# Five of eight state products on GpSimd, row replication in fp32, residual and biases on TensorE

## The chip, the cores and the metric

One core of a Trainium2 chip runs the whole program in one launch. Its engines are TensorE (PE, matmuls from SBUF to PSUM), VectorE (DVE), ScalarE (ACT), GpSimd (POOL) and SyncE (SP, which issues most DMAs). The metric is the time of one execution on the device in microseconds; lower is better.

## The reference

The input is x of 2 x 16 x 16 x 64, so 2 batches of 256 tokens with 64 features. Six layers follow one another: an edge attention with an MLP, a group-normalised attention, an attention with 8 heads, a mixture of 8 experts with top 2, six state-space layers, and a second mixture. The change touches the six state-space layers (and small pieces of work that are slipped in before them):

```python
def selective_scan(u, dt, A, Bm, Cm, Dp):
    def step(h, inp):
        u_t, dt_t, B_t, C_t = inp
        h = jnp.exp(dt_t[..., None] * A) * h + (dt_t * u_t)[..., None] * B_t[:, None, :]
        y_t = jnp.einsum('bds,bs->bd', h, C_t)
        return (h, y_t)
    ...
def mamba_mixer(x, in_w, cw, cb, xp_w, dt_w, dt_b, A_log, Dp, out_w):
    xz = x @ in_w
    u, z = jnp.split(xz, 2, axis=-1)
    uc = silu(causal_conv4(u, cw) + cb)
    x_dbl = uc @ xp_w                            # 16 for dt, 16 for B, 16 for C
    dt = jax.nn.softplus(dt_r @ dt_w + dt_b)
    A = -jnp.exp(A_log)
    y = selective_scan(uc, dt, A, Bm, Cm, Dp)
    y = y * jax.nn.silu(z)
    return y @ out_w
for i in range(6):
    residual = hidden if residual is None else hidden + residual
    hidden = rmsnorm(residual, norm_w[i])
    hidden = mamba_mixer(hidden, ...)
```

Inner width is 128 channels, the state has 16 entries per channel, the sequence is 256 steps.

## The kernel before

Every engine has its own instruction stream, written out by hand, and semaphores order the streams. The state-space part is twelve *units* u = 0 to 11, unit u being layer u // 2 of batch u % 2. The two batches alternate, so that while the scans of unit u run, unit u+1 is prepared. Units 0 and 9 to 11 are written out; units 1 to 8 come from a loop of two turns over four units.

A unit holds 16 states, taken in four groups g of four states: a group is a tile of 128 channels x (4 x 256). For each group there is a *drive* product (dt times u, times B, replicated over the channels), a scan over 1024 columns with the decay factors, and a *weighing* product with C. Eight products thus.

- DVE (`v_step`): `prep_dt` (L1091: two polynomial steps L1098, a product L1102, dt L1105, dtu L1108), `gate` of the unit before (L1085), drive of group 0 (L1121, B from PSUM), `residual` of the unit before (L1089), four scans (L1133), and the weighings of groups 0, 2 and 3 (L1140, C from PSUM); `prep_uc` of the next unit (L1078) stands after the third scan.
- POOL (`p_step`): drives of groups 1 to 3 (L1611, B from a DMA broadcast), weighing of group 1 (L1619), and small operations for the next unit: the root mean square, the scaling of the hidden state (L1567), gz (L1576), parts of softplus's polynomial (L1597, L1600), and the rounding remainders (L1582, L1588).
- PE (`pe_step`): B and C must be replicated over 128 channels. The kernel holds them as three bf16 parts stacked on 96 rows and multiplies with a picking matrix: `spread_b` (L634) and `spread_c` three times (L643), each four matmuls of 256 columns into two PSUM banks (4 and 5). `sum_y` (L664) adds the weighed states in PSUM by fp32 matmuls with the identity, sixteen a unit; `sum_skip` (L650) adds D times u. `prep_transpose`, `prep_in`, `prep_x` and `prep_dt` (L609 to L627) prepare the next unit; `out_proj` (L672) is the output projection; `keep_awake(3)` (L655) are three matmuls without use.
- ACT (`a_step`): sixteen decay exponentials (L1405), the norm's squares (L1353), ht in two halves (L1361), two sigmoids by tanh (L1368, L1373), copies xds and stack (L1377, L1379), softplus: abs, relu, exp and four squares (L1385 to L1391), and the middle part of the stack (L1397).
- SP: per unit it writes xds to a scratch tensor in device memory and reads it back as four broadcasts to 128 partitions (three groups of B, group 1 of C), 512 KB each; and it reloads one layer's weights every second unit.

An fp32 matmul shows as two records on PE. PE, DVE, ACT and POOL each run their stream in order.

Of the kernel before, what the change touches and what calls it, by code (L numbers as in the profile page):

```python
# [19 lines left out]
P = 128  # L20
# [15 lines left out]
LOG1P = np.polynomial.Polynomial(  # L36
    np.polynomial.chebyshev.Chebyshev.interpolate(
        lambda u: np.log1p(u) / np.maximum(u, 1e-300), 8, domain=[0, 1]).convert(
        kind=np.polynomial.Polynomial).coef)

def quadratics():
    roots = LOG1P.roots()
    upper = sorted((r for r in roots if r.imag > 0), key=lambda r: r.real)
    k2 = float(LOG1P.coef[-1]) ** (1.0 / len(upper))
    k = k2 ** 0.5
    return [(k, -k * r.real, k2 * r.imag ** 2) for r in upper]
# [29 lines left out]
def hybrid(nc, x, const, w0, w1, w2, w3, w5, wm, rows, out):  # L77
    ctx = ExitStack()
    with ctx:
# [3 lines left out]
        spill = nc.dram_tensor("spill", (B, DS + SG, N), F32, kind="Internal").ap()  # L83
# [12 lines left out]
        wmt = [sb(f"wmt{k}", [P, WM.size]) for k in range(2)]  # L96
# [14 lines left out]
        pick_b = sb("pick_b", [P, 32], BF16)  # L111
# [76 lines left out]
        bsp = halves(0, (DS - SG) * N, N)  # L188
        dbu = big[:, 8192:12288].rearrange("p (g s n) -> p g s n", g=NSG, s=SG)
        hst = halves(12288, SG * N, N) + halves(22528, SG * N, N)  # L190
        csp = halves(20480, SG * N, N)

        hc = big[:, 16384:20480].rearrange("p (g s n) -> p g s n", g=NSG, s=SG)
        sp_q = halves(14336, 4 * N, N)
        sg, zs = two("sg", [P, 2, N]), two("zs", [P, N])
        uc, gz, dt, dtu, yg = (two(n, [P, N]) for n in ("uc", "gz", "dt", "dtu", "yg"))
        sp_u, sp_m = PS[:, 7, 0:N], two("sp_m", [P, N])
        ht = two("ht", [P, N + 4])
        hs2 = two("hs2", [P, HALF, P])
        xds, stack = two("xds", [P, N]), two("stack", [P, N], BF16)  # L200
        rest = sb("rest", [64, N])
        wcv, alog, amat = two("wcv", [P, 2 * P]), two("alog", [P, DS]), two("amat", [P, DS])
        dmat = two("dmat", [P, P])
        ssq, msq, rms = two("ssq", [P, 2]), two("msq", [P, 2]), two("rms", [P, 2])
        hbias = two("hbias", [P, 1])
        half_t, power_t = sb("half_t", [P, 1]), sb("power_t", [P, 1])
        sqs = sb("sqs", [P, HALF, D])
        eps_t, eps2_t, zero_t, quad_t = sb("eps_t", [P, 1]), sb("eps2_t", [P, 1]), sb("zero_t", [P, 1]), sb("quad_t", [P, 8])
# [3 lines left out]
        yps, idle_ps = PS[:, 6, 0:N], PS[:, 6, N:2 * N]  # L212
        ups, xd = PS[:, 7, 0:N], PS[0:112, 7, 0:N]
        tr, zps, dtp = (PS[:, 7, N:2 * N] for _ in range(3))
# [6 lines left out]

        def layer_loaded(eng, i, s):

            eng.wait_ge(sem(f"ld_wm{(s // 2) % 2}"), i * 16 + 16 * (s // 4 + 1))
# [5 lines left out]
        def _(sp):  # L230
# [22 lines left out]
            for u in range(UNITS):  # L253
                n, b = u // 2 + 1, u % 2
                if b == 1 and 2 <= n < NL:
                    sp.wait_ge(sem("m_hid"), 2 * n - 2)
                    sp.dma_start(wmt[n % 2][:], wm[n]).then_inc(sem(f"ld_wm{n % 2}"), 16)
                sp.wait_ge(sem("m_xds"), u + 1)
                sp.dma_start(spill[b], xds[b][SG:DS + 2 * SG, :]).then_inc(sem("st_B"), 16)
                sp.wait_ge(sem("st_B"), 16 * (u + 1))  # L260
                for g in range(1, NSG):
                    rows_of = spill[b, SG * (g - 1):SG * g].rearrange("s n -> (s n)")
                    sp.dma_start(bsp[b][:, SG * (g - 1):SG * g].rearrange("p s n -> p (s n)"),
                                 rows_of.partition_broadcast(P)).then_inc(sem(f"ld_B{b}{g}"), 16)
                rows_of = spill[b, DS:DS + SG].rearrange("s n -> (s n)")
                sp.dma_start(csp[b][:].rearrange("p s n -> p (s n)"),
                             rows_of.partition_broadcast(P)).then_inc(sem(f"ld_C{b}"), 16)
# [8 lines left out]
        def _(pe):  # L276
# [74 lines left out]
            spare(7, 2)  # L351
            to_T2(Y, PS[:, 2, 0:N], "ln_out", 1, "turned")
            pe.wait_ge(sem("turned_sb"), 2)
            by_batch(lambda b: PS[:, 5 + b, 0:N], lambda r: W0.of(w0t, "w1")[r], T2b).then_inc(sem("f0_h"), 1)
# [17 lines left out]
            spare(7, 2)  # L372

            to_T2(X, PS[:, 3, 0:N], "ln_out", 2, "turned")
            spare(7, 1)
# [229 lines left out]
            def prep_transpose(u, k, b):  # L606
                pe.wait_ge(sem("m_hs"), u + 1)
                for a in range(HALF):
                    last = pe.transpose(tr[:, a * P:(a + 1) * P], hs2[b][:, a], ident)  # L609
                last.then_inc(sem("m_tr"), 1)  # L610

            def prep_in(u, k, b, layers):
                pe.wait_ge(sem("m_ht"), u * 2 + 2)
# [11 lines left out]
            def prep_dt(u, k, b):  # L625
                pe.wait_ge(sem("m_xds"), u + 1)
                pe.matmul(dtp, WM.of(wmt[k], "dtw")[96:112], xds[b][96:112], start=True, stop=True).then_inc(sem("m_dtp"), 1)  # L627
# [1130 lines left out]
```

## Time and profile before

| | us |
|---|---|
| median of 3 runs | 408.72 (407.43 to 410.31) |
| span of the profiled execution | 409.9 |
| PE busy | 340.5 |
| DVE busy | 314.7 |
| ACT busy | 249.1 |
| POOL busy | 210.6 |
| mean granted clock of TensorE | 0.926 of 2.4 GHz |

The page has a busy time and an instruction count for each engine, then the groups of instructions by line. The timeline gives each instruction's start, its duration, and what the engine idled for just before it. The profile is of one execution, the slowest core's (there is only one). The state-space units lie between about 145 and 381 us; before them come the edge attention, the attentions and the first mixture, after them the second mixture.

### The profile page before, as it was taken

Reading aid. Unit: us, or ns where it says so; the run is one execution under the profiler, and the core shown is the slowest. Engines: PE = TensorE matmul, PEld = TensorE weight load, DVE = VectorE, ACT = ScalarE, POOL = GpSimd, SP = SyncE. Lnnn points to the kernel's source line nnn. Section 1 sums busy time; section 2 is a strip of 40 time slices with the busy share of each in tenths; the row PEclk is TensorE's granted clock in tenths of the full one; section 3 lists DMA queues with packets and bytes.
Section 4 is the critical chain, followed back from the end, with each engine's and each line's share of the span. In section 5 each row is a group of like instructions: output and inputs, shape, how many; then the busy total and the mean of one; then the engine's idle time right before and its main releaser. Section 6 shows DMA issues by size and latency. Waiting matters only on the chain.

```text
span 409.9 us, 5884 instructions
## 1 busy us (share of the span) xinstructions
PE 340.5 (83%) x1818; PEld 235.1 (57%) x1818; DVE 314.7 (77%) x538; ACT 249.1 (61%) x681; POOL 210.6 (51%) x235
## 2 busy tenths in 40 slices
PE   5868998999899986888887979888888879768674
PEld 3356765565584654566664757566566647557442
DVE  2674678898653618779999799979988999998653
ACT  2012378888727455948778586948676786862170
POOL 1985000000000028788889698868977797882000
PEclk9985999999979997899999899899989999987868
DMA  7900000000002105142450515161342326050000
GB/s 238 403 7 1 2 1 2 0 2 2 0 2 64 40 4 206 44 165 75 173 178 31 208 43 205 29 220 62 144 162 86 123 86 210 3 203 0 2 0 13
DMA packets 11345, 35.24 MB, mean 86 GB/s; under 512 B 2368, under 2 KB 2992, under 8 KB 11192
## 3 DMA queue, kind: packets, MB, share of 16 engines
q1 hardware_dynamic: 11032, 34.61, 23.9%
q10 hardware_dynamic: 288, 0.33, 0.3%
q8 instruction: 12, 0.20, 0.2%
q14 instruction: 13, 0.11, 0.1%
HBM read 34.54 MB, written 0.39 MB: 85 GB/s over the span
## 4 chain that ended last, share of the span: by engine, by line
PE 53%; DVE 24%; ACT 12%; issue 5%; DMA 3%; POOL 2%; DVEq 0%; SPq 0%; POOLq 0%; ACTq 0%
PE PS L664 15%; DVE big L1133 7%; ACT PS L1405 4%; PE PS L511 4%; PE PS L643 3%; DVE big L1121 3%; DVE big L1140 3%; PE PS L475 2%; ACT sg L1368 2%; PE PS L289 2%; PE PS L295 2%; PE PS L627 2%; PE PS L405 2%; PE PS L575 2%; PE PS L485 2%
## 5 line engine op out<-in xcount | busy, mean ns | idle before, releaser
L1133 DVE TENSOR_TENSOR_SCAN big<-PS,big 128x1024 f32<-128x1024 f32 x48 | 109.3, 2284 | 3.0 <-ACT PS L1405 2.7
L664 PE MATMUL PS<-big,cst 128*128 128x256 f32 x384 | 96.0, 407 | 0.0
L1405 ACT ACTIVATE PS<-dt,amat 128x255 f32<-128x255 f32 x192 | 80.1, 466 | 25.4 <-DVE dt L1105 21.5
L1611 POOL TENSOR_TENSOR big<-dtu,big 128x1024 f32<-128x1024 f32 x36 | 84.2, 2356 | 7.2 <-DVE dtu L1108 6.6
L664 PEld LDWEIGHTS PS<-big,cst 128*128 128x128 f32 x384 | 76.8, 205 | 14.9 <-issue 3.7
L1644 POOL TENSOR_SCALAR lnv<-mv 128x4 f32<-128x4 f32 x1 | 0.4, 418 | 93.9 <-DVE mv L770 93.9
L1140 DVE TENSOR_TENSOR big<-big,PS 128x1024 f32<-128x1024 f32 x36 | 43.8, 1216 | 0.9
L1239 ACT ACTIVATE big<-PS 128x512 f32<-128x512 f32 (+1 forms) x43 | 24.8, 584 | 22.3 <-PE PS L511 7.3
L643 PE MATMUL PS<-stack,pick_b 96*128 96x256 bf16 x144 | 23.9, 292 | 17.0 <-DVE big L1140 9.2
L1286 ACT ACTIVATE big<-PS,big 128x256 f32<-128x256 f32 x64 | 29.8, 475 | 1.5 <-DVE big L902 1.5
L1619 POOL TENSOR_TENSOR big<-big 128x1024 f32<-128x1024 f32 x12 | 28.3, 2358 | 1.1 <-DVE big L1133 1.1
L643 PEld LDWEIGHTS PS<-stack,pick_b 96*128 96x128 bf16 x144 | 11.8, 102 | 27.0 <-DVE big L1140 12.5
L902 DVE TENSOR_REDUCE big<-PS 128x2 f32<-128x512 f32 x32 | 22.0, 688 | 6.5 <-PE PS L405 3.1
L655 PE MATMUL PS<-cst 128*128 128x256 f32 x102 | 26.2, 396 | 0.0
L511 PE MATMUL PS<-cst,big 128*128 128x128 f32 x128 | 20.9, 285 | 3.2 <-ACT big L1239 1.9
L1597 POOL TENSOR_TENSOR big<-big,quad_t 128x256 f32<-128x256 f32 x24 | 14.2, 612 | 15.5 <-ACT big L1391 15.5
L511 PEld LDWEIGHTS PS<-cst,big 128*128 128x128 f32 x128 | 13.5, 140 | 14.4 <-DVE big L911 6.9
L655 PEld LDWEIGHTS PS<-cst 128*128 128x128 f32 x102 | 19.0, 198 | 3.0 <-issue 0.7
L911 DVE TENSOR_SCALAR big<-big 128x256 f32<-128x256 f32 x64 | 19.7, 350 | 1.1
L1391 ACT ACTIVATE big<-PS,quad_t 128x256 f32<-128x256 f32 x48 | 18.9, 477 | 0.4
L295 PE MATMUL PS<-cst 128*128 128x256 f32 x62 | 18.7, 436 | 0.0
L1361 ACT ACTIVATE ht<-PS,wmt 64x256 f32<-64x256 f32 x24 | 11.3, 471 | 12.1 <-PE PS L609 11.8
(309 smaller groups left out, 624.6 us busy)
## 6 DMA issues: line engine op xcount, KB each, us to landing
big<-spill SPq DMA_DIRECT2D x48, 512.0 KB, 5.6
wmt<-in_wm SPq DMA_DIRECT2D x6, 418.0 KB, 3.2
w3t<-in_w SPq DMA_DIRECT2D x1, 1588.0 KB, 13.5
big<-routed SPq DMA_DIRECT2D x8, 128.0 KB, 3.0
w2t<-in_w SPq DMA_DIRECT2D x1, 896.0 KB, 10.1
cst<-in_const SPq DMA_DIRECT2D x1, 848.0 KB, 8.0
w5t<-in_w SPq DMA_DIRECT2D x1, 812.0 KB, 15.0
w1t<-in_w SPq DMA_DIRECT2D x1, 385.0 KB, 8.4
```

What stands on the lines that cost most here:

```text
L295: pe.matmul(PS[:, bank, N:2 * N], ident, CONST.of(cst, "rope")[:, 0:N], start=True, stop=True)
L511: last = pe.transpose(PS[:, 6 + t, m * N + a * P:m * N + (a + 1) * P], probs[:, i % SLOTS, a, m * P:(m + 1) * P], ident)
L643: last = pe.matmul(PS[:, 4 + c, s * N:(s + 1) * N], pick_b[0:96, col:col + 1].to_broadcast([96, P]), stack[b][0:96], start=True, stop=True)
L655: pe.matmul(idle_ps, ident, CONST.of(cst, "rope")[:, 0:N], start=True, stop=True)
L664: last = pe.matmul(yps, ident, hc[:, g, s], start=False, stop=(g == NSG - 1 and s == SG - 1))
L1133: v.tensor_tensor_scan(flat(hst[g][:]), flat(da[g % 2]), flat(dbu[:, g]), 0.0, ALU.mult, ALU.add).then_inc(sem("m_h"), 1)
L1140: v.tensor_tensor(hc[:, g], hst[g][:], BCv, ALU.mult).then_inc(sem("m_hc"), 1)
L1239: copy = lambda dst, src, **kw: act.activation(dst, src, ACT.Copy, **kw)
L1286: act.activation(probs[:, i % SLOTS, a], PS[:, i % 4, a * N:(a + 1) * N], ACT.Exp, bias=rowmax[:, i, a:a + 1], accum_out=rowsum[:, i, a:a ...
L1405: one = act.activation(da[g % 2][:, n, 1:N], dt[b][:, 1:N], ACT.Exp, scale=amat[k][:, col:col + 1])
L1611: pool.tensor_tensor(dbu[:, g], dtu[b][:].unsqueeze(1).to_broadcast([P, SG, N]), bsp[b][:, SG * (g - 1):SG * g], ALU.mult).then_inc(sem("m ...
L1619: pool.tensor_tensor(hc[:, 1], hst[1][:], csp[b][:], ALU.mult).then_inc(sem("m_hc_pool"), 1)
```

## The change

- POOL computes five of the eight products: drives of groups 2 and 3 and weighings of groups 0, 1 and 2. DVE has drives 0 and 1 and the weighing of group 3, in two halves. SP broadcasts five tiles per unit in place of four.
- B and C are replicated by fp32 matmuls from 32-row slices of xds, which holds both twice, on rows 0 to 31 and 32 to 63. The bf16 stack, its rounding and the operations for it go. There are three replications a unit.
- dt's matmul uses the product of the two weight matrices, computed once (wdt), and starts from uc and not from xds. The biases of the convolution and of dt enter PSUM by a bf16 matmul of three parts with ones. silu(uc) is (tanh + 1) times u with a factor of 0.5 folded into the weights.
- softplus: log1p(exp(-|x|)) becomes a form of tanh and squares; ACT does abs, exp, tanh and three squares, DVE three fused steps, POOL nothing.
- The residual is added by PE into the PSUM tile of the output projection, ACT copies it back (`keep_residual`); ACT also scales the hidden state; ht is written in one operation, because PE places the shifted copy.
- All six layers' weights are loaded early, in pieces, and prepared by POOL, PE and ACT during earlier stages. PE waits for one of these loads (`ld_wr`). The loops are written out, and the three idle matmuls per unit are gone.

```diff
@@ @block.sync
-            for k in range(2):
-                sp.dma_start(wmt[k][:], wm[k]).then_inc(sem(f"ld_wm{k}"), 16)
+            sp.dma_start(wr[:], part("xp", 96)).then_inc(sem("ld_wr"), 16)
+            sp.dma_start(dtw, part("dtw")[96:96 + RANK]).then_inc(sem("ld_wr"), 16)
+            for to, name, n in ((wxd[:], "xp", D), (wout[:], "out", D), (cols[:], "alog", DS + 4)):
+                sp.dma_start(to, part(name, 0, n)).then_inc(sem("ld_ms"), 16)
...
+            for n in range(3):
+                sp.dma_start(braw[32 * n:32 * n + 1].rearrange("o (i p t) -> o i p t", i=NL, t=2),
+                             wm[:, :, at:at + 2].unsqueeze(0)).then_inc(sem("ld_brow"), 16)
...
+                for g in range(5):
+                    to = bsp[b][:, SG * g:SG * (g + 1)] if g < 2 else csp[b][:, SG * (g - 2):SG * (g - 1)]
+                    sp.dma_start(to.rearrange("p s n -> p (s n)"),
+                                 spill[b, SG * g:SG * (g + 1)].rearrange("s n -> (s n)").partition_broadcast(P))
@@ @block.tensor
-            spare(7, 2)
+            pe.wait_ge(sem("ld_wr"), 32)
+            for n in range(NL):
+                last = pe.transpose(PS[0:RANK, 4 + n // 4, (n % 4) * P:(n % 4 + 1) * P], wr[:, n], ident)
...
+            def prep_x(u):
+                i, b = divmod(u, 2)
+                pe.wait_ge(sem("m_uc"), u + 1)
+                pe.matmul(dtp, bias[:, i, :, 1], ones[:], start=True, stop=False)
+                pe.matmul(dtp, wdt[:, i], uc[b], start=False, stop=True)
+                pe.matmul(xd, wxd[:, i], uc[b], start=True, stop=True).then_inc(sem("m_xd"), 1)
+            def replicate(u, first):
+                b = u % 2
+                for s in range(2):
+                    for c in range(2):
+                        r = slice(32 * c, 32 * c + 32)
+                        col = first + 2 * c + s
+                        last = pe.matmul(PS[:, 4 + c, s * N:(s + 1) * N], pick[r, col:col + 1].to_broadcast([32, P]),
+                                         xds[b][r], start=True, stop=True)
+                last.then_inc(sem("m_BC"), 1)
...
+            for u in range(UNITS):
+                more = u + 1 < UNITS
+                if u:
+                    sum_y(u - 1, 2)
+                    sum_last(u - 1)
+                spread_first(u)
+                if u:
+                    out_proj(u - 1)
+                spread_second(u)
+                if more:
+                    prep_transpose(u + 1)
+                    prep_in(u + 1)
+                spread_last(u)
+                if more:
+                    prep_x(u + 1)
+                sum_skip(u, u + 1 if more else None)
+                sum_y(u, 0)
+                sum_y(u, 1)
@@ @block.vector
+            def prep_dt(u):
+                v.scalar_tensor_tensor(sp_a, sp_3, LOG_D2, sp_u, ALU.add, ALU.mult)
+                v.scalar_tensor_tensor(sp_v, sp_2, LOG_SCALE * LOG_D, sp_a, ALU.add, ALU.mult)
+                v.scalar_tensor_tensor(dt[b], dtp, 0.0, sp_v, ALU.max, ALU.add)
+                v.scalar_tensor_tensor(dtu[b], dt[b], 0.5, uc[b], ALU.mult, ALU.mult)
...
+            for u in range(UNITS):
+                prep_dt(u)
+                if u:
+                    gate(u - 1)
+                drive(u, 0)
+                scan(u, 0)
+                drive(u, 1)
+                scan(u, 1)
+                if u + 1 < UNITS:
+                    prep_uc(u + 1)
+                scan(u, 2)
+                scan(u, 3)
+                weigh_last(u)
@@ @block.scalar
+            def prep_softplus(u):
+                act.activation(sp_a, dtp, ACT.Abs)
+                act.activation(sp_u, sp_a, ACT.Exp, scale=-1.0)
+                act.activation(sp_v, sp_a, ACT.Tanh, scale=0.5, bias=turn_t)
+                act.activation(sp_3, sp_u, ACT.Square, bias=a2_t)
+                act.activation(sp_1, sp_v, ACT.Square, bias=a_t)
+                act.activation(sp_2, sp_1, ACT.Square, scale=LOG_ROOT, bias=b_t)
...
+                decay(u, 0, every)
+                if u:
+                    act.wait_ge(sem("m_hid"), u)
...
+                if more:
+                    prep_norm(u + 1)
+                if u:
+                    keep_residual(u - 1)
+                decay(u, 1, every[0:2])
+                if more:
+                    prep_hs(u + 1)
+                decay(u, 1, every[2:4])
+                if more:
+                    prep_ht(u + 1)
+                decay(u, 2, every[0:3])
+                if more:
+                    prep_tu(u + 1)
+                decay(u, 2, every[3:4])
+                if more:
+                    prep_zs(u + 1)
+                decay(u, 3, every)
+                if more:
+                    prep_xd(u + 1)
+                    prep_softplus(u + 1)
+                    prep_z(u + 1)
@@ @block.gpsimd
+            for u in range(UNITS):
+                more = u + 1 < UNITS
+                drive(u, 2)
+                if more:
+                    prep_rms(u + 1)
+                drive(u, 3)
+                for g in range(3):
+                    weigh(u, g)
+                if more:
+                    prep_gz(u + 1)
```

(Semaphore calls and blank lines are left out in parts of the quoted diff.)

## Rows read from the trace of the kernel before

**Rows 1.** The page, busy us, share of the span and instructions of each engine.
```profile
PE 340.5 (83%) x1818; PEld 235.1 (57%) x1818; DVE 314.7 (77%) x538; ACT 249.1 (61%) x681; POOL 210.6 (51%) x235
```

**Rows 2.** Windows: stretch, its length, busy us of PE, PEld, DVE, ACT, POOL, clock, DMA.
```profile
200.00:240.00 40.00, 33.69 (x154) 23.98 (x153) 36.67 (x35) 28.87 (x80) 33.44 (x32) 0.96 0.34 118
```

**Rows 3.** Timeline of DVE, one unit: start us, duration us, line, operation, idle before.
```profile
233.77 0.42 DVE L1085 TENSOR_TENSOR yg<-PS,gz 128x256 f32<-128x256 f32 x1 [2.25 <-PE PS L664]
234.21 1.22 DVE L1121 TENSOR_TENSOR big<-dtu,PS 128x1024 f32<-128x1024 f32 x1
...
235.55 2.29 DVE L1133 TENSOR_TENSOR_SCAN big<-PS,big 128x1024 f32<-128x1024 f32 x1
237.88 1.22 DVE L1140 TENSOR_TENSOR big<-big,PS 128x1024 f32<-128x1024 f32 x1
239.01 4.51 DVE L1133 TENSOR_TENSOR_SCAN big<-PS,big 128x1024 f32<-128x1024 f32 x2
...
250.22 0.42 DVE L1105 TENSOR_TENSOR dt<-PS,sp_m 128x256 f32<-128x256 f32 x1
250.68 0.84 DVE L1108 TENSOR_TENSOR dtu<-dt,uc 128x256 f32<-128x256 f32 x1
251.58 0.42 DVE L1085 TENSOR_TENSOR yg<-PS,gz 128x256 f32<-128x256 f32 x1
```

**Rows 4.** Timeline of PE, the end of the same unit.
```profile
246.19 5.35 PE L664 MATMUL PS<-big,cst 128*128 128x256 f32 x24
251.38 0.60 PE L634 MATMUL PS<-stack,pick_b 96*128 96x256 bf16 x4
```

**Rows 5.** Chain that ended last, 160 to 375 us: start, us, what.
```profile
171.56 6.87 PE PS L664 x24
```

**Rows 6.** The line L1085 and what its engine waited for before it (us, times).
```profile
  PE PS L664: 10.1, 7
```

**Rows 7.** Timeline of DVE, the first gate and the last two.
```profile
178.47 0.42 DVE L1085 TENSOR_TENSOR yg<-PS,gz 128x256 f32<-128x256 f32 x1 [1.70 <-PE PS L664]
...
362.85 0.42 DVE L1085 TENSOR_TENSOR yg<-PS,gz 128x256 f32<-128x256 f32 x1 [0.55 <-PE PS L664]
...
379.74 0.42 DVE L1085 TENSOR_TENSOR yg<-PS,gz 128x256 f32<-128x256 f32 x1 [1.77 <-issue]
```

**Rows 8.** Timeline of PE in the attention, scores of 32 rows.
```profile
72.79 1.13 PE L405 MATMUL PS<-big 32*128 32x256 f32 x8
73.86 0.66 PE L511 MATMUL PS<-cst,big 128*128 128x128 f32 x4
```

**Rows 9.** Groups by line and form: busy us, mean ns, idle before.
```profile
L1391 ACT ACTIVATE big<-PS,quad_t 128x256 f32<-128x256 f32 x48 | 18.9, 477 | 0.4
...
L1353 ACT ACTIVATE sqs<-Y 128x64 f32<-128x64 f32 x22 | 5.5, 249 | 17.8 <-DVE Y L1089 17.8
```

**Rows 10.** Timeline of POOL, a root mean square and a weighing.
```profile
236.60 0.71 POOL L1563 TENSOR_TENSOR rms<-msq,power_t 128x2 f32<-128x2 f32 x1
...
242.58 2.38 POOL L1619 TENSOR_TENSOR big<-big 128x1024 f32<-128x1024 f32 x1
```

**Rows 11.** Windows of 1 us, columns as rows 2; the last is GB/s.
```profile
250.50:251.50 1.00, 1.00 (x7) 0.78 (x6) 0.97 (x2) 0.65 (x2) 1.00 (x3) 1.00 1.09 442
```

**Rows 12.** DMA issues of the page: KB each, us from issue to landing.
```profile
w3t<-in_w SPq DMA_DIRECT2D x1, 1588.0 KB, 13.5
```

**Rows 13.** Timeline of DVE, entry into unit 0.
```profile
144.43 0.42 DVE L1065 TENSOR_TENSOR hs<-Y,rstd 128x256 f32<-128x256 f32 x1 [1.27 <-POOL rstd L1646]
...
157.49 1.22 DVE L1121 TENSOR_TENSOR big<-dtu,PS 128x1024 f32<-128x1024 f32 x1
```

**Rows 14.** Windows of PE alone: busy us, clock, DMA share, GB/s.
```profile
160.00:163.00 3.00, 3.00 (x8) 0.50 0.02 10
```

**Rows 15.** Timeline of DVE and POOL, two operations that start together.
```profile
287.94 1.01 DVE L1108 TENSOR_TENSOR dtu<-dt,uc 128x256 f32<-128x256 f32 x1
287.94 0.72 POOL L1544 TENSOR_TENSOR wcv<-wmt 128x256 f32<-128x256 f32 x1
```

More of the change, by code:

```diff
@@ L198, in hybrid @@
+        uc, gz, dt, dtu, yg, tu, zs, zt = ([unit_t[:, N * (2 * n + t):N * (2 * n + t + 1)] for t in range(2)]
+                                           for n in range(8))
         ht = two("ht", [P, N + 4])
         hs2 = two("hs2", [P, HALF, P])
[L200 to L203, printed above, removed]
+        xds = two("xds", [64, N])
@@ L371, in _ @@
             last.then_inc(sem("a_w"), 1)
-            spare(7, 2)
+            for n in range(NL):
+                last = pe.matmul(PS[:, 7 - n // 2, N + (n % 2) * P:N + (n % 2 + 1) * P], wrT[:, n], dtw[:, n],
+                                 start=True, stop=True)
+            last.then_inc(sem("m_wp"), 1)
             to_T2(X, PS[:, 3, 0:N], "ln_out", 2, "turned")
+            pe.wait_ge(sem("m_wdt"), 3)
             spare(7, 1)
@@ L708, in _ @@
-            keep_awake(7)
-            prep_transpose(0, 0, 0)
-            keep_awake(1)
-            prep_in(0, 0, 0, 1)
-            keep_awake(4)
-            prep_x(0, 0, 0)
-            keep_awake(1)
-            prep_dt(0, 0, 0)
-            keep_awake(5)
-            pe_step(0, 0, first=True)
-            with pe.Fori(0, 2) as i:
-                for s in range(1, 5):
-                    pe_step(i, s)
-            for s in range(9, 12):
-                pe_step(0, s, last=(s == 11))
-            sum_y(UNITS - 1, 1, NSG - 1)
@@ L724, in _, with keep_awake @@
-            out_proj(UNITS - 1, 1, 1)
+            def keep_awake(count, bank=5):
+                for _ in range(count):
+                    pe.matmul(PS[:, bank, N:2 * N], ident, CONST.of(cst, "rope")[:, 0:N], start=True, stop=True)
+            keep_awake(7, 6)
+            prep_transpose(0)
+            keep_awake(1)
+            pe.wait_ge(sem("m_weights"), 5)
+            prep_in(0)
+            keep_awake(3)
+            prep_x(0)
+            keep_awake(7)
+            for u in range(UNITS):
[16 more added lines that the diff above has]
+                sum_y(u, 1)
@@ L1437, in _, with prep_norm @@
[L1437 to L1447 removed]
+            def prep_norm(u):
+                b = u % 2
+                for a in range(HALF):
+                    last = act.activation(sqs[:, a], hidp[:, a] if u >= 2 else Y[:, a, b], ACT.Square, scale=D ** -0.5,
+                                          accum_out=ssq[b][:, a:a + 1])
+                last.then_inc(sem("m_ssq"), 1)
@@ new lines, in keep_residual, with prep_hs, prep_ht @@
+            def keep_residual(u):
+                act.activation(Y[:, :, u % 2], hidp, ACT.Copy).then_inc(sem("m_ycp"), 1)
+            def prep_hs(u):
+                b = u % 2
+                act.wait_ge(sem("m_rms"), u)
+                for a in range(HALF):
+                    last = act.activation(hs2[b][:, a, 0:D], hidp[:, a] if u >= 2 else Y[:, a, b], ACT.Copy,
+                                          scale=rms[b][:, a:a + 1])
+                last.then_inc(sem("m_hs"), 1)
+            def prep_ht(u):
+                act.wait_ge(sem("m_tr"), u + 1)
+                act.activation(ht[u % 2][:, 3:3 + N], ups, ACT.Copy, scale=cols[:, u // 2, DS + 3:DS + 4])\
+                    .then_inc(sem("m_ht"), 1)
```

622 lines of the change are left out of this document (245 added, 377 removed).

## The prediction

> **What bounds the kernel now.** I read the page first: PE is busy 83% and DVE 77% of the span [rows 1]. A mean over stages decides nothing, so I went on to the stages. In the middle of the twelve units of the state-space layers, 200 to 240 us, DVE is busy 36.7 of 40 us, PE 33.7, POOL 33.4, ACT 28.9 [rows 2]. DVE and PE are both near full there; a change has to relieve both.
>
> The timeline of one unit at full clock shows the cycle. From gate to gate (L1085, start 233.77 and 251.58) it is 17.8 us [rows 3]. DVE's part: five operations for dt and dtu (0.46 each from start to start), gate, one drive product (1.22), four scans (two in a row take 4.51, so 2.23 from start to start; 2.33 before a product that needs the scan), three weighing products (237.88 to 239.01, 1.13 each), uc. PE's part: after the last C replication come twelve fp32 matmuls against the identity, 24 records, issued in 5.19 us (246.19 to 251.38), 0.433 each, and the gate starts 0.04 us after they end [rows 4]. So both chains are 17.8 long. In four of the units these 24 records took 6.5 to 6.9 us, as in the row at 171.56 [rows 5]: part of them ran at TensorE's lower level, 1.2 GHz. Then DVE waits at the gate, 10.1 us in seven units together [rows 6]. The mean period is thus 18.4: (362.85 - 178.47) / 10 [rows 7].
>
> **The change, part by part.** I lay the new unit out with T = 0 where the last sum of the unit before ends, at full clock, and ask when the next one ends.
>
> *fp32 rows spread.* Four bf16 replications per unit (about 0.45 issued each [rows 4]) become three in fp32 from 32-row slices, alternating between two row groups and two banks. Before has no such spread, but its attention scores have this form: four logical fp32 matmuls of 32 rows and 256 columns, alternating row groups, are issued in 1.07 us (72.79 to 73.86) [rows 8]. If the groups did not overlap it would be 4 x 0.433 = 1.73. I take 1.07: same shape, same alternation. The rounding work goes away: ACT's two copies, POOL's rest and low.
>
> The Trainium skill (TensorE: Matmul & The Clock Gate, Part 3) has different row groups start about 4 ns apart; by it two pairs would cost 0.87. The row is slower than that and decides; by the rule the unit would be 0.2 us shorter.
>
> *DVE.* First spread issued by 0.97; gate 0.04 to 0.46 runs beside it; drive 0 from 1.0 to 2.25. The scan after a dependent product starts 1.34 after the product did (234.21 to 235.55) [rows 3]: scan 0 at 2.35 to 4.64. Drive 1 is new on DVE: 4.66, scan 1 5.94 to 8.2, uc to 8.64, scan 2 8.6, scan 3 10.8 to 13.1, then the last weighing in two halves to 14.4. Two weighings and the residual leave DVE, one drive comes: saved 2 x 1.13 + 0.2 - 1.28 = 1.2. prep_dt has four operations instead of five: 14.35 to 16.15. So DVE alone is ready for the next gate at 16.15.
>
> *PE.* out_proj, two fp32 matmuls of 64 columns, 0.2 to 0.6 with its latency (four bf16 ones of 256 columns take 0.60 [rows 4]), plus 0.22 for the residual (a 128-column fp32 identity matmul, half of 0.433) end by 1.9 at the latest, in the shadow of drive 0. Second spread 2.29 to 3.36. Hidden state: ACT norm two squares of 0.25 [rows 9], then keep_residual; POOL msq and rms about 1.0, rms alone 0.71 [rows 10]; ACT's scaling, two operations again, about 0.5: hs at 4.4, after two exponentials that ACT puts in between. The transposes are now two plus two fp32 matmuls of 128 columns: below 0.4, if all overlap like the row-group pairs, above 1.3, if each of the five weight loads shows; I take 1.0, to 5.4 (less gains nothing, since prep_x waits for uc; 1.3 costs 0.1 a unit). ht is one ACT operation of 0.48 (two today), prep_in 0.11 + 3 x 0.433 from 6.0 to 7.4 (the bias as bf16 matmul of 96 rows costs what one of the replications costs). Third spread to 8.47. prep_x needs uc, 8.68: 0.11 + 2 x 0.433 to 9.65. Then skip and sixteen sums, 17 x 0.433 = 7.36: the last ends at 17.1. That is the unit: 8.6 of DVE, then 8.4 of PE. DVE waits 0.95 at the gate.
>
> *POOL, the 5 of 8 products.* 2.36 each [rows 10]: drive 2 up to 1.4; rms to 3.65; drive 3 to 6.0; weigh 0 to 8.4, weigh 1 to 10.7, weigh 2 after scan 2, 10.84 to 13.2. The sums of group 2 start at 13.55, so it hides, with 0.35 us to spare. Sum 5 x 2.36 + 0.98 + 0.73 = 13.5, less than today's 15 with quartic, rest, low, hs.
>
> *ACT, log1p by tanh and squares.* Six operations of 0.37 to 0.48 (a square: 0.477 [rows 9]) for softplus, from 10.45 to 13.0, z to 13.8; DVE asks for them at 14.35. Hidden, and 1.35 late next if it slips. Today's extra round xds, dt matmul, ACT is gone, because the two weights are multiplied beforehand.
>
> *Broadcasts.* Five of 512 KB per unit instead of four: issued from 11.9, at the 442 GB/s of the trace's fullest stretch 5.9 us, at half of that 12 [rows 11]; the first two are wanted at 16.2 and 21, the three C at 23 and later. Hidden.
>
> *Weights early.* Small-descriptor loads go behind w3t, and PE waits for one of them (wr) near 28 us; w3t lands 13.5 us after its issue, at about 18 [rows 12]; even 8 us for the small ones is in time. Two `spare(7, 2)` (0.87 us each at full clock) give way to transposes and small matmuls of like length. POOL has nothing else to do between 50 and 140 us, so its new operations there cost nothing. I put 0, bounds -0.5 and +1.5.
>
> *Entry.* Today hs is ready at 144.85 and drive 0 starts at 157.49 [rows 13]. New: hs, transposes, ht 146.25; tu 148.0; uc 148.5; PE is held by three idle matmuls to 149.1; x 150.1; xds 150.5; softplus 152.95; dt 153.9; drive 0 at 154.4, so T = 153.4, 3.1 us earlier.
>
> *Sum.* First gate: 153.4 + 17.1 + 1.0 (PE ran at 0.50 over 160 to 163, in the first unit [rows 14]; a like start is likely) = 171.5, against 178.47. Ten units: 171, and 7 for falls of the clock: four of the ten units lose 1.3 to 1.7 today [rows 5], and the new unit hangs on the sums in the same way. Gate 10 at 349.5 against 362.85. Last unit: no preparation; 16.5 against 16.9, gate at 366.0 against 379.74 [rows 7]. Behind it keep_residual on ACT takes the place of the residual on DVE, +0.05. 409.9 - 13.7 = 396.2 for the profiled execution. Its span is 1.2 above the median run, 408.72; so 395 for the median.
>
> **Rivals.**
> (A) *The row groups do not overlap.* The first and third spread are on the path, with 0.2 of slack: +1.15 a unit, 12 units, +14: 409. Against it speaks the row of the scores [rows 8]. 0.05.
> (B) *POOL's products collide with DVE's.* Place: prep_dt. Three of its four operations now read two SBUF tensors (before one, dtu: 0.42 alone, 1.01 when a POOL operation with two inputs ran beside it [rows 15]). With my times POOL is in gz (to 14.5) when prep_dt begins at 14.35. If POOL is more than 1.15 us later than I have it, weigh 2 still runs and sp_a waits it out, up to 2.36, and dtu behind gz about 0.4 more; less the 0.95 of slack, 1.8 a unit, +22: 417. It eats the whole gain (13.7 / 12 = 1.14 a unit) from a delay of 1.15 + 0.95 + 1.14 - 0.4 = 2.8 us. POOL's order (drive 3 behind rms) speaks for it, the scan 2 that paces weigh 2 against it. 0.08.
> (C) *The clock falls more often*, since the three keep_awake per unit are gone and PE still idles some 2 us a unit. If each unit lost 1.7 instead of four of eleven: +12: 407. The busy share rises (PE idles 0.4 before the second spread, 1.1 and 0.6 around the transposes, 0.2 before prep_x: 14.8 of 17.1 = 87%, against 84% [rows 2]), which speaks against it. 0.12.
> (D) *The clock falls less*, and the sums never meet a fall, as in six of the ten periods today: -7, 388. 0.2.
> (E) The forecast, 395, own range 390 to 402: 0.55.
>
> **Numbers.** What a measurement here can tell from no change is about 1%, 404.6 to 412.8. Faster: E, D and a little of C, 0.8. Same: A and most of C, 0.12. Slower: B, 0.08. Low end 386: D with replications at 0.87. High end 408: C and A; above lies B.
>
> **What would show it.** Gate to gate 17.1 in undisturbed units; DVE idle about 1 us before the gate, released by PE's sums; four spread matmuls issued in 1.07 us; POOL's weigh 2 ends before prep_dt begins; the sp operations last 0.43 and not 1 to 2 us; drive 0 of unit 0 near 154.4. Wrong if POOL's third weighing ends after the second group of sums (PE waits for it), if the spread takes 1.7, if PE waits for wr near 28 us, or if the granted clock in 160 to 350 is below 0.9.

## The result, and the profile after

The changed kernel takes 471.5 us (median of 4 runs, 469.2 to 472.7) against 408.7: a ratio of 1.155, interval 1.147 to 1.163. The prediction was 395 (386 to 408), so it had the sign wrong.

| | before | after |
|---|---|---|
| span of the profiled execution, us | 409.9 | 470.2 |
| hs of unit 0 computed on DVE | 144.43 | 157.61 |
| drive 0 of unit 0 | 157.49 | 169.40 |
| first gate | 178.47 | 193.69 |
| mean period, gate to gate, of ten units | 18.44 | 22.85 |
| last gate | 379.74 | 439.4 |

The page of after, busy time, share and instructions of each engine; to be read beside [rows 1]:

```profile
PE 408.7 (87%) x1978; PEld 271.0 (58%) x1978; DVE 308.6 (66%) x514; ACT 235.8 (50%) x653; POOL 205.4 (44%) x159
```

PE's busy time grew by 68 us though its instructions grew by 160 only; the other engines' busy time fell. Stretches of after, PE alone: length, busy us, granted clock, DMA share, GB/s:

```profile
200.00:240.00 40.00, 37.84 (x134) 0.68 0.32 117
240.00:280.00 40.00, 36.72 (x148) 0.74 0.23 87
320.00:360.00 40.00, 37.28 (x159) 0.80 0.37 133
400.00:440.00 40.00, 35.19 (x151) 0.79 0.21 84
```

The clock stands at 0.68 to 0.80 where before had 0.96 [rows 2]. DVE's gates, one unit apart, with the idle time ahead of each in brackets:

```profile
263.13 0.42 DVE L1112 TENSOR_TENSOR unit_t<-PS,unit_t 128x256 f32<-128x256 f32 x1 [3.14 <-PE PS L690]
...
280.30 0.89 DVE L1106 SCALAR_TENSOR_TENSOR unit_t<-unit_t 128x256 f32<-128x256 f32 x1
285.66 0.42 DVE L1112 TENSOR_TENSOR unit_t<-PS,unit_t 128x256 f32<-128x256 f32 x1 [4.47 <-PE PS L690]
```

DVE waits 3.1 to 4.7 us for PE's sums at every gate, where before waits 10.1 us in seven units together [rows 6]. Now PE in this unit:

```profile
263.02 1.13 PE L651 MATMUL PS<-xds,cst 32*128 32x256 f32 x8
264.09 0.49 PE L700 MATMUL PS<-Y,cst 128*128 128x128 f32 x2
...
265.48 1.13 PE L651 MATMUL PS<-xds,cst 32*128 32x256 f32 x8 [0.51 <-DVE big L1119]
267.18 0.28 PE L619 MATMUL PS<-cst,zero_t 128*64 128x1 f32 x2 [0.56 <-ACT hs L1372]
...
269.20 0.28 PE L629 MATMUL PS<-ones,bias 96*128 96x256 bf16 x1 [0.57 <-ACT ht L1379]
...
272.05 2.08 PE L651 MATMUL PS<-xds,cst 32*128 32x256 f32 x8
274.05 0.39 PE L638 MATMUL PS<-ones,bias 96*128 96x256 bf16 x1
...
277.29 6.61 PE L683 MATMUL PS<-big,cst 128*128 128x256 f32 x24
```

The first spread takes 1.13 and is issued in 1.07 (263.02 to 264.09), the third, the same eight records, takes 2.08 and is issued in 2.00 (272.05 to 274.05). The granted clock of the same unit:

```profile
263.00:269.00 6.00, 4.56 (x31) 1.00 0.36 146
269.00:270.00 1.00, 0.80 (x4) 0.80 0.00 0
270.00:279.00 9.00, 9.00 (x25) 0.50 0.01 2
279.00:280.00 1.00, 1.00 (x4) 0.58 0.44 180
280.00:285.00 5.00, 5.00 (x25) 1.00 0.81 327
```

Full speed (2.4 GHz) until 269.6, then half (1.2 GHz) for 10.2 us: the windows with 0.80 and 0.58 hold 0.4 and 0.84 us of the low level, and nine lie between. Such a stretch at half speed is called a fall here. What ran ahead of it were two 32-row spreads, a 64-column projection, transposes of 128 columns, and three waits. At half speed 10.2 us do the work of 5.1 at most, so without the fall this unit, 22.54 long from first spread to first spread, would have taken 17.4 or somewhat more. Every one of the ten units has such a fall. It lasts 10.2 us in six of them and 13.7 in four, whose periods are 23.7, and it starts 4.2 to 6.5 us behind the gate. The kernel before has falls of 3.4 us, in three of its ten periods and once ahead of the first gate.

The rest of the loss comes before the layers. DVE in the weight stage, then POOL in the same stretch:

```profile
37.46 2.46 DVE L802 TENSOR_TENSOR X<-X,mv 128x256 f32<-128x256 f32 x1
39.96 1.57 DVE L804 TENSOR_TENSOR X<-X,rowt 128x256 f32<-128x256 f32 x1
41.56 1.57 DVE L792 TENSOR_TENSOR X<-X,rstd 128x256 f32<-128x256 f32 x1
43.16 3.19 DVE L808 TENSOR_TENSOR X<-X,rowt 128x256 f32<-128x256 f32 x1
```

```profile
36.55 3.09 POOL L1561 TENSOR_TENSOR unit_t<-big,bias 96x1536 f32<-96x1536 f32 x1
39.71 3.14 POOL L1564 CAST bias<-unit_t 32x1536 bf16<-32x1536 f32 x2
42.93 3.14 POOL L1566 TENSOR_TENSOR unit_t<-unit_t,bias 32x1536 f32<-32x1536 f32 x1
```

Operations of 0.42 us take 1.6 to 3.2, and each ends 0.3 us after an operation of POOL's new weight preparation. T2a, the normalised input of the attention (L880), comes at 51.92 where before has it at 43.20, and the attention scores start at 57.30 instead of 47.54.

### The profile page after: what moved, and what is told of

It reads as the page before. It is cut to its first block, busy times and chain, and to the rows that moved or that the text cites. A ratio compares the mean times of both kernels' runs of the same rounds, so it can differ in the third digit from the quotient of the medians.

```text
span 470.2 us, 5816 instructions
## 1 busy us (share of the span) xinstructions
PE 408.7 (87%) x1978; PEld 271.0 (58%) x1978; DVE 308.6 (66%) x514; ACT 235.8 (50%) x653; POOL 205.4 (44%) x159
## 3 DMA queue, kind: packets, MB, share of 16 engines
q1 hardware_dynamic: 19464, 40.29, 24.7%
## 4 chain that ended last, share of the span: by engine, by line
PE 74%; DVE 11%; ACT 6%; POOL 4%; issue 3%; DMA 2%; DVEq 0%; POOLq 0%; SPq 0%; ACTq 0%
PE PS L683 15%; PE PS L651 8%; PE PS L690 4%; PE PS L520 3%; PE PS L677 3%; PE PS L632 3%; PE PS L622 3%; PE PS L640 3%; PE PS L639 2%; PE PS L631 2%; PE PS L630 2%; PE PS L484 2%; PE PS L414 2%; PE PS L296 2%; PE PS L290 2%
## 5 line engine op out<-in xcount | busy, mean ns | idle before, releaser
L1615 POOL TENSOR_TENSOR big<-big 128x1024 f32<-128x1024 f32 x36 | 84.4, 2347 | 20.0 <-issue 12.8
L1425 ACT ACTIVATE PS<-unit_t,amat 128x255 f32<-128x255 f32 x192 | 81.5, 468 | 5.2 <-DVE big L1128 2.8
L683 PEld LDWEIGHTS PS<-big,cst 128*128 128x128 f32 x288 | 64.8, 225 | 12.1
L1606 POOL TENSOR_TENSOR big<-unit_t,big 128x1024 f32<-128x1024 f32 x24 | 57.5, 2397 | 15.5 <-DMA big<-spill 15.5
L651 PE MATMUL PS<-xds,cst 32*128 32x256 f32 x288 | 53.0, 497 | 9.9 <-DVE big L1119 9.9
L651 PEld LDWEIGHTS PS<-xds,cst 32*128 32x128 f32 x288 | 31.0, 232 | 26.8 <-DVE big L1119 12.2
L1243 ACT ACTIVATE big<-PS 128x512 f32<-128x512 f32 (+1 forms) x43 | 24.7, 583 | 25.4 <-PE PS L520 10.0
L1112 DVE TENSOR_TENSOR unit_t<-PS,unit_t 128x256 f32<-128x256 f32 x12 | 5.1, 424 | 48.2 <-PE PS L690 45.5
L1119 DVE TENSOR_TENSOR big<-unit_t,PS 128x1024 f32<-128x1024 f32 x24 | 29.0, 1208 | 7.2 <-PE PS L651 7.1
L1597 POOL TENSOR_TENSOR unit_t<-unit_t 128x256 f32<-128x256 f32 x12 | 8.7, 726 | 50.1 <-ACT unit_t L1398 50.1
L926 DVE TENSOR_SCALAR big<-big 128x256 f32<-128x256 f32 x64 | 19.7, 350 | 1.1
L690 PEld LDWEIGHTS PS<-big,cst 128*128 128x128 f32 x96 | 18.2, 190 | 2.5
L1403 ACT ACTIVATE xds<-PS 64x256 f32<-64x256 f32 x12 | 4.5, 377 | 27.5 <-PE PS L640 27.5
```

The lines of the kernel that those rows point to most:

```text
L651: last = pe.matmul(PS[:, 4 + c, s * N:(s + 1) * N], pick[r, col:col + 1].to_broadcast([32, P]), xds[b][r], start=True, stop=True)
L683: pe.matmul(yps, ident, hc[:, g, s], start=False, stop=False)
L690: last = pe.matmul(yps, ident, hc[:, NSG - 1, s], start=False, stop=(s == SG - 1))
L1119: v.tensor_tensor(dbu[:, g], dtu[u % 2].unsqueeze(1).to_broadcast([P, SG, N]), BCv, ALU.mult)\
L1243: copy = lambda dst, src, **kw: act.activation(dst, src, ACT.Copy, **kw)
L1425: one = act.activation(da[g % 2][:, n, 1:N], dt[u % 2][:, 1:N], ACT.Exp, scale=amat[:, u // 2, col:col + 1])
```

## The experiments

Times in one group share a chip and the runs of before (medians of 411.4 to 412.5 us there); the ratios are against these. e7, e8 and e11 are of two runs each. Line numbers shift by a few where lines were added.

### The weight stage: is it POOL's products beside DVE's?

**e2: the products later.**

```diff
+            pool.wait_ge(sem("g_x"), 1)
             pool.wait_ge(sem("ld_brow"), 48)
```

> The changed kernel, with POOL's preparation of the weights (casts and differences of the biases, from 35.0 us on) held back until DVE has written the normalised input of the second attention, when DVE's chain of 96 to 128 partition operations with two SBUF inputs is over. Theory 1, DVE's operations there were stretched by POOL's long two-input ones (2.46, 1.57, 1.57 and 3.19 us against 0.42): they fall back to 0.42, the scores start 9 to 10 us earlier (at 47.5 to 48), time about 462. Rival, the stretch is a clash with the weight loads by DMA, which still run: durations stay, time 471.

Measured: 471.5, ratio 1.143. DVE's four operations are back at 0.42 and the scores start at 51.72, but others are now long:

```profile
53.49 2.95 DVE L991 TENSOR_TENSOR X<-X,rowt 128x256 f32<-128x256 f32 x1
57.27 2.52 DVE L926 TENSOR_SCALAR big<-big 128x256 f32<-128x256 f32 x2
```

hs of unit 0 comes at 156.4 instead of 157.6. The expected gain didn't come: moved later, POOL's block of products meets DVE in the attention instead.

**e6: the same products in pieces of 128 columns**, in the same place.

```diff
-            pool.tensor_tensor(brest, braw, raw, ALU.subtract)
+            cut(lambda c: pool.tensor_tensor(brest[:, c], braw[:, c], raw[:, c], ALU.subtract))
```

(and so for the other six long ones)

> The changed kernel with POOL's long operations on the weights cut into pieces of 128 columns, same work, same place. e2_pool_late showed that the collision with DVE only moves if the work is held back (L991 2.95, L926 1.26 each beside POOL, sum unchanged at 471.5). If a long POOL operation makes DVE wait for its end, short ones make each DVE operation wait at most some 0.3 us: L802 to L808 at 0.5 to 0.8 in place of 2.46 to 3.19, scores start near 49 in place of 57.3, time about 463. If instead the two engines share the port by halves, DVE is slowed as long as POOL works, and the time stays at 471.

Measured: 465.0, ratio 1.128; scores at 49.68, hs at 148.6, 9.0 us earlier than in after. One of POOL's operations, now twelve pieces, then DVE's same ones:

```profile
35.11 3.18 POOL L1565 CAST bias<-big 96x128 bf16<-96x128 f32 x12
```

```profile
36.79 1.35 DVE L802 TENSOR_TENSOR X<-X,mv 128x256 f32<-128x256 f32 x1
38.17 0.42 DVE L804 TENSOR_TENSOR X<-X,rowt 128x256 f32<-128x256 f32 x1
38.63 0.53 DVE L792 TENSOR_TENSOR X<-X,rstd 128x256 f32<-128x256 f32 x1
```

So the stretch came from the length of POOL's operations, not from DVE's own work or a late load. L802 is the exception: at 1.35 it lasts longer than any single piece (0.27 each), and why it waits over several of them stays open. Of after's 9.8 us at the scores this gives back 7.6. The periods stay at 22 to 24, so it is a loss apart from the units'.

Not all of the 13.2 us at hs is the change's. With the early code of after untouched, hs came at 154.8 to 158.5 in six executions; with that of before at 144.4, 144.5 and 148.7, and TensorE's clock falls differently ahead of hs each time; that this makes the difference is likely but was not tested. The profile of before has one of the early ones. The same holds for e6: against those six its 148.6 is 6.2 to 9.9 us earlier, and its whole time is 6.5 us shorter than after's.

### The unit: what lowers the clock?

Theory R: full-row matmuls are missing from the first part of a unit (the 96-row replications became 32-row ones, and the three idle matmuls went). Theory G: the three waits of 0.5 us alone do it. Theory W: it is just the amount of work.

**e1: three idle matmuls (128 rows, 256 columns) ahead of the transposes.**

```diff
                 spread_second(u)
                 if more:
+                    pe.wait_ge(sem("m_zs"), u + 1)
+                    keep_awake(3, 6)
                     prep_transpose(u + 1)
```

> The changed kernel, with three matmuls without use per unit (fp32 against the identity, 256 columns) put back, between the second replication and the transposes. Theory 1, PE's clock falls in every unit because the stretch from the first replication to the transposes keeps PE too little at work (1.0 clock until 269, 0.50 from 270 to 280 in the profile of the changed kernel): gates 17 to 19 us apart in place of 22.8, mean granted clock above 0.88, time 471 - 11 x 4 = about 427 or less. Theory 2, the clock is taken back because PE works too much (87% busy): the clock stays at 0.79 or below and the time is 471 or a few us more. Theory 3, it is the kind of matmul (32 rows), not the idle time: the fall stays in most units, 460 to 475.

Measured: 427.2, ratio 1.035 (1.026 to 1.045): 44 us less by adding work. Periods 18.57, two of 20.1, stretches of 40 us at 0.91 to 1.00:

```profile
240.00:280.00 40.00, 37.85 (x181) 0.91 0.38 132
280.00:320.00 40.00, 37.84 (x195) 1.00 0.41 143
```

The two longer periods hold one fall of 3.4 us each; the other eight have none.

**e3: e1 and e2 together.**

> Both of the above. If the two losses are separate, the gains add: 427 - 9.5 = about 417 (or less, if the idle matmuls restore the clock wholly: down to 405). If the clock's phase ties them, the sum is off by more than 3 us.

Measured: 431.6, ratio 1.046; periods 18.57, hs at 156.0. Nothing from e2 again, as its own run had it.

**e8: e1, but each of the three reads 32 rows.** Same place, same count, same columns.

```diff
-                    keep_awake(3, 6)
+                    for s in range(3):
+                        pe.matmul(PS[:, 6, N:2 * N], ident[0:32], CONST.of(cst, "rope")[0:32, 0:N], start=True, stop=True)
```

> As e1_awake3 (same place, three matmuls of 256 columns, so the same time), but each uses 32 rows of the array in place of 128. If the clock goes by PE's time at work, the result is e1's: about 427. If rows of the array count, the clock falls in every unit as in the changed kernel: 471 to 490, and the 32-row replications are then a cause of the fall by their kind.

Measured: 485.0, ratio 1.178 (1.163 to 1.191): 58 us more than e1, and more than after. PE in one unit:

```profile
243.30 2.76 PE L731 MATMUL PS<-cst 32*128 32x256 f32 x6
...
252.06 2.08 PE L651 MATMUL PS<-xds,cst 32*128 32x256 f32 x8
```

```profile
240.00:280.00 40.00, 37.84 (x145) 0.67 0.23 86
```

Three such matmuls take 2.7 us where full clock has 1.3. The clock is 1.00 until 243.2 and 0.50 from 243.3 on, so in this unit it falls just as they start; e1 has falls at the same place, 3.3 and 3.7 us behind the gate. What differs is how often and how long: e1 has a fall of 3.4 us in two of its ten periods, e8 one in all ten, of 10.2 to 17.1 us. The wait ahead of the transposes is gone, as in e1, and the clock is no better than in after. So theory G alone can't hold, nor theory W: what differs from e1 is the rows.

**e7: three full-row idle matmuls ahead of the skip product**, where PE has no wait.

> The changed kernel with the three idle matmuls put where PE is busy anyhow, between prep_x and the skip product. Same number and kind as e1_awake3 (427). If what matters is PE's work in the stretch before the transposes, the clock still falls in every unit and the time is 471 + 11 x 1.3 to 2.6, so 480 to 500. If only the number of full matmuls per unit matters, 427 to 435.

Measured: 479.9, ratio 1.165; periods 23.8. The same three matmuls that gave 44 us in e1 cost 8 here: the clock is already at 0.5 when they run. This speaks against theory W.

**e11: the spreads read 64 rows**, nothing idle added.

```diff
-                        r = slice(32 * c, 32 * c + 32)
+                        r = slice(0, 64)
```

(and 64 in place of 32 where the picking column is broadcast). B and C are then wrong, sums of the two halves, so this run stands for its time alone.

> The changed kernel with the three replications reading 64 rows of the stack in each matmul instead of 32 (the values of the two halves are then added, so B and C are not the reference's; no idle matmuls). Their matmuls no longer run side by side: a replication of four takes 4 x 0.43 = 1.7 us instead of 1.07, so TensorE has 1.9 us more work a unit at full clock. Theory R (the clock falls because 32 rows keep little of the array at work): the fall shortens or goes, periods 18 to 20 and total 420 to 445 although there is more to do. Theory G (the gaps alone, 0.5 us each, bring the fall): periods stay at 22.9 or grow by up to 1.9, total 471 to 490.

Measured: 447.8, ratio 1.087 (1.080 to 1.094). PE, then gates, then a stretch:

```profile
252.99 1.99 PE L651 MATMUL PS<-xds,cst 64*128 64x256 f32 x8
...
256.29 1.99 PE L651 MATMUL PS<-xds,cst 64*128 64x256 f32 x8 [0.50 <-DVE big L1119]
```

```profile
253.10 0.42 DVE L1112 TENSOR_TENSOR unit_t<-PS,unit_t 128x256 f32<-128x256 f32 x1 [2.71 <-PE PS L690]
272.55 0.43 DVE L1112 TENSOR_TENSOR unit_t<-PS,unit_t 128x256 f32<-128x256 f32 x1 [2.71 <-PE PS L690]
```

```profile
240.00:280.00 40.00, 37.30 (x172) 1.00 0.36 133
```

A spread takes 1.92 instead of 1.07 from start to start, 2.5 us more work in a unit, and the unit is 3.4 us shorter: 19.45, in nine of ten periods (the tenth is 25.5), with two of the three waits still there. That is theory R's number. This run alone mixes two things, rows and the longer time that the spreads take; e8 against e1 changes the rows alone and says the same.

**e5: one idle matmul in each of the three waits.**

```diff
                     out_proj(u - 1)
+                pe.wait_ge(sem("m_zs"), u + 1)
+                keep_awake(1, 6)
                 spread_second(u)
                 if more:
+                    keep_awake(1, 6)
                     prep_transpose(u + 1)
+                    keep_awake(1, 6)
                     prep_in(u + 1)
```

> The changed kernel with three idle matmuls per unit, as in e1_awake3, but one in each of the three waits of PE (0.51 us before the second replication, 0.56 before the transposes, 0.57 before prep_in), where they should cost nothing at full clock. If it is the idle time that lets the clock fall, it does not fall at all, or as rarely as in the kernel before: gates 17.8 apart, time 411 to 418. If three in a row are needed, the clock falls in some units: 425 to 450.

Measured: 415.6, ratio 1.007 (1.002 to 1.013). Gates, and a stretch:

```profile
244.56 0.43 DVE L1116 TENSOR_TENSOR unit_t<-PS,unit_t 128x256 f32<-128x256 f32 x1 [1.52 <-PE PS L690]
262.27 0.42 DVE L1116 TENSOR_TENSOR unit_t<-PS,unit_t 128x256 f32<-128x256 f32 x1 [1.52 <-PE PS L690]
```

```profile
240.00:280.00 40.00, 39.95 (x203) 1.00 0.49 169
```

All ten periods are 17.71 or 17.72, the clock is 1.00 from 200 to 360 us. PE from prep_in's start (L629) to the next first spread:

```profile
250.63 0.28 PE L629 MATMUL PS<-ones,bias 96*128 96x256 bf16 x1
...
262.16 1.13 PE L651 MATMUL PS<-xds,cst 32*128 32x256 f32 x8
```

These are 11.53 us, where after has 16.36 for the same matmuls (269.20 to 285.56). So the fall of 10.2 us costs 4.83, and 22.54 - 4.83 = 17.71. It is less than half of the fall's length because not all of the time doubles: a spread is issued in 1.07 at full and 2.00 at half speed. The clock accounts for the whole of the period's growth: (22.85 - 17.71) x 10 = 51 us.

### What the idle matmuls were worth in the kernel before

**e4: the kernel before without its `keep_awake(3)`.**

> The kernel before, with its three matmuls without use per unit taken out and nothing else. Theory 1: PE then idles 1.3 us more between the first C replication and the transposes, the clock falls in all or nearly all units, and the period goes from 18.4 to about 21: time 408.7 + 11 x 2.5 = 430 to 440. Theory 2 (too much work): fewer falls, 400 to 408. Theory 3 (kind of matmul): no change within 2 us.

Measured: 432.6, ratio 1.055 (1.047 to 1.063). Gates from 177.40 to 380.95 in ten periods, 20.4 each; clock 0.74 to 0.83. The clock falls in all ten, for 6.8 us in six and 10.2 in four, though the replications here read 96 rows: fewer full-row matmuls suffice for a fall, without the 32-row ones. Two of after's 4.4 us a unit come with these three matmuls alone, in the old code; with them back in the new code (e1) 18.57.

**e10: the kernel before with two more** (one ahead of the wait for drive 0, four instead of three).

> The kernel before with two more idle matmuls per unit: one ahead of the wait for the first drive product (a gap of 0.58 us), and four instead of three ahead of the skip product. Theory (any cleared gap holds the clock): the 4 falls in 10 units, which cost 4 x 1.4 us by the periods (17.8 undisturbed, 19.2 with a fall), vanish: 5 to 6 us off, about 403 to 406 where before has 409 to 411. Rival (TensorE in the kernel before is near its bound, and 0.86 us more work per unit goes into the period): 10 x 0.3 to 0.8 us longer, 412 to 418.

Measured: 410.1, ratio 0.997 (0.9945 to 1.0003). Its falls went from three to two in ten periods (these two are 19.6, the others 17.8 to 18.1), and gates 1 to 11 span 182.1 instead of 184.4 us. But hs of unit 0 came at 148.7. Neither expectation held: the added matmuls cost nothing, one fall went, and what was won is within what the stages ahead vary. Whether this version gains is open. The expectation counts four falls, and so does the prediction; the fourth long period of before, 18.60 up to the gate at 344.98, is none. There the clock is 1.00, and PE waits longer for the next unit's hidden state, 0.97 us where the units around it have 0.2 to 0.4:

```profile
320.00:360.00 40.00, 33.78 (x162) 1.00 0.33 116
```

```profile
331.40 0.44 PE L609 MATMUL PS<-cst,hs 128*128 128x128 f32 x2 [0.97 <-POOL hs L1567]
```

### A version from both repairs

**e9: e5 and e6 together.**

> Both repairs at once: one idle matmul in each of TensorE's three waits (it gave 415.6 alone, periods of 17.71), and GpSimd's long weight products cut into pieces of 128 columns (alone it brought the first residual projection input 9.0 us earlier and 6.5 us of the total). Theory (two independent losses, an early one on VectorE's shared operand path and one per unit from TensorE's clock): the gains add, periods stay 17.71 and the first input of the layers comes at about 149 instead of 154.9, total 407 to 410 against 411 to 412 for the kernel before: equal to it or 1% faster. Rival (the early gain is eaten by the clock, which also falls in attention): total stays at 414 to 416.

Measured: 409.5, ratio 0.994 (0.990 to 0.997); periods 17.71, hs at 150.2. The two gains add.

**e12: e9 with idle matmuls of 192 columns.**

```diff
-                keep_awake(1, 6)
+                keep_awake(1, 6, 192)
```

> Both repairs with idle matmuls of 192 instead of 256 columns. In the version with 256 columns each idle matmul keeps TensorE 0.63 to 0.68 us where the wait it stands in for was 0.51, 0.56 and 0.57 us, and TensorE is busy 39.95 of 40 us, so the period of 17.71 holds 1.95 us of idle matmuls for 1.64 us of waits. At 192 columns one takes about 0.48 us and fits into each wait. Theory (TensorE's chain alone sets the period, and the clock holds with the short ones too): 17.71 - (1.95 - 1.64) = 17.4 a unit, 3.4 us less in 11, total about 406 against 409.5, ratio 0.985 to 0.99. Rival (the uncovered 0.1 us of each wait, or the narrower products, let the clock fall again in some units): some periods of 19 to 23 us, total 415 or more.

Measured: 407.0, ratio 0.991 (0.986 to 0.995), the fastest here, by a margin under 1%. The expected period of 17.4 didn't come; it is 17.71 as with 256 columns, and the intervals of e9 and e12 overlap. PE of e12:

```profile
254.68 0.56 PE L703 MATMUL PS<-wout,unit_t 128*128 128x64 f32 x4
255.07 0.54 PE L709 MATMUL PS<-cst 128*128 128x192 f32 x2
255.75 1.13 PE L651 MATMUL PS<-xds,cst 32*128 32x256 f32 x8
```

From the idle matmul's start to the spread's is 0.68 us, which is what it was with 256 columns. The "idle before" of a PE row (0.51) counts from the modelled end of the record ahead, so the wait from start to start is longer than it reads, and idle matmuls of 256 columns had filled it without lengthening it. 17.71 is the unit's own length at full clock.

## Why the prediction was wrong

In the profiled execution it missed by 470.2 - 396.2 = 74.0 us. By its own milestones: first gate 22.2 late (193.69 for 171.5), ten periods 50.5 longer (228.5 for 178), the last unit and the tail 1.3.

**The clock term was the failed step.** It put 7 us for falls in ten units, from the kernel before, "and the new unit hangs on the sums in the same way"; measured are 51. The mechanism stood there as rival C, but at 0.12 and at 1.7 a unit, while a fall of 10.2 us costs 4.83 and the mean unit lost 5.1. Three things went wrong:
- The price was copied from before's falls of 3.4 us, and their number from the four long groups of sums. One of these, at 171.56 [rows 5], lies ahead of the first gate, so three fell in the ten periods. The new fall comes in every unit and lasts three to four times as long.
- What spoke against it was the busy share, 87% against 84%. It is a mean over the unit. In the first 6 us after the last sum, PE is busy 4.46 us before (251.4 to 257.4) and 4.56 after (263 to 269), about the same. Then the clock falls for 10.2 us in the kernel after; in the kernel before it stays at 1.00 until 264.0. The share said nothing of the fall, over the unit or over this stretch.
- The three idle matmuls were named as removed and priced at nothing. e4 shows their price in the kernel before, 2 us a unit. What no row of before could show is the part of the rows: in its units only dt's product ran on few rows, 16, once a unit, and the scores of [rows 8], on 32, were read for their issue time alone.

The stretch of before that the second point reads, to be laid beside after's 263.00:269.00:

```profile
251.40:257.40 6.00, 4.46 (x27) 1.00 0.33 135
```

The Trainium skill (TensorE: Matmul & The Clock Gate, Part 1) explains the low level by how busy TensorE has lately been, and the runs here don't bear that out unless rows count towards it: e1 and e8, 427 and 485 us, add the same three matmuls with 128 or 32 rows.

**Weights early at 0 (-0.5 to +1.5) was the second.** POOL's idle 50 to 140 us was taken as cover, though the new work runs at 35 to 53, beside DVE's norms. The collision itself was on the page: [rows 15] served for rival B, placed at prep_dt only. Of the 13.2 us at hs, e6 gives back 9.0 (6.2 to 9.9, as said there). The Trainium skill (SBUF — State Buffer, Who interferes with whom) has an exclusive lock between a DVE instruction with two SBUF inputs and a POOL instruction that reads SBUF. L802's 2.46 us beside 3.09 on POOL agrees; its 1.35 beside pieces of 0.27 in e6 is more than one piece's length. The section counts TENSOR_SCALAR, in some of its forms, among the operations that can be held up too; L926 in e2 is one, at 2.52 for two.

**The unit at full clock: 17.71, not 17.1.** The order was right and DVE waits for PE's sums as said, but longer, 1.52 for 0.95. From e5's PE starts: prep_in 1.71 for 1.41, prep_x 1.22 for 0.97, skip and sums 7.54 for 7.36, the first half 6.18 for 6.0. The step that failed is "0.433 each": that is the pitch inside a run of equal matmuls. From L631 to L632 it is 0.52, from L640 to L677 0.57, from L632 to the spread 0.63: a change of form adds 0.1 to 0.2. This term makes 6 of the 50.5 us, the clock the other 44. And at 17.71 against 17.8 [rows 3] the rearrangement saves 1 us in ten units, where 17.1 would have saved 7: most of the expected gain wasn't there even with the clock intact.

**Entry.** 3.1 us was claimed from hs to drive 0; measured 11.8 against 13.1, so 1.3. And the first unit took 24.3 us from drive 0 to its gate, not 17.1 (171.5 - 154.4): PE ran at half speed for 17.1 us of it (0.76 over 160 to 200). The idle matmuls did not cure this one: e5 has the same 17.1 us and 24.7 there, e9 6.8 us and 21.0. What decides between them stays open.

**Right:** row groups do overlap (1.07; rival A out). POOL and ACT are hidden; POOL's weigh 2 ends before prep_dt, of whose three operations with two SBUF tensors the first two last 0.43 (rival B out); only dtu pays, 0.89 beside gz, inside DVE's slack. POOL's drive 2 waits 15.5 us for broadcasts in 12 units, also hidden: PE sets the period in each run of the new code. The prediction's own test, "wrong if the granted clock in 160 to 350 is below 0.9", was the one that came true. Rival D (388) fell with the unit's length: no run had a period under 17.7.

## What to carry to other kernels

Before taking away matmuls that compute nothing, or making matmuls narrower in rows, price the clock for the stretch behind them, in every repetition: a fall costs nearly half of its length where TensorE has no wait in it (4.83 for 10.2 us here). A high busy share was no cover. Idle matmuls belonged into the waits ahead of the place where the clock falls, not where TensorE has work. And weight preparation that is "off the path" on GpSimd has to be laid beside VectorE's timeline of those very microseconds; if they meet, cut it in short pieces.

## What the hardware showed beyond what was expected

- Matmuls of 32 rows did not keep TensorE's clock up: three idle ones of 128 rows gave 427 us, of 32 rows in the same place 485. With replications of 64 rows instead of 32 the clock was 1.00 over 200 to 280 us, with 2.5 us more work a unit and 24 us less in all. What exactly about the rows counts stays open.
- One idle matmul in each of three waits left no fall in ten periods, at 17.71; three in one place left two falls of 3.4 us (periods of 20.1). Without a fall that version's period is 18.57, and the 0.86 is the time of the idle matmuls themselves, which outlast the one wait they stand in.
- A fall of 10.2 us cost 4.83 us, a little less than half: a spread takes 1.07 at the full level and 2.00 at the low one.
- DVE's wait behind a POOL operation follows POOL's length: DVE operations of 0.42 took 1.6 to 3.2 us beside ones of 1536 columns, and 0.42 to 0.64 (once 1.35) beside pieces of 128.
- TensorE's pitch in a run of equal fp32 matmuls is 0.433, and 0.52 to 0.63 where the next one has another form.
